# A graph layer's own features, stored to DRAM and added by block in place of a transposed copy

## The reference

```
h = relu(layernorm(x)); x = x + layer0(h)   # edge-weighted sum over neighbours, then two linear maps
h = relu(layernorm(x)); x = x + layer1(h)

# layer1(feat):
m = relu(feat[src]) + EPS
a = exp(m - segment_max) / segment_sum(exp)     # softmax over the edges that end in a node, per feature
msg = segment_sum(a * m, dst)
return (feat + msg) @ W + b
```

## Time and profile before

| | us |
|---|---|
| median of 3 runs | 2506.68 (2506.21 to 2509.19) |
| the profiled execution | 2505.36 |
| its span, first to last instruction | 2503.60 |
| mean granted clock of TensorE | 0.874 of full speed |
| busy: TensorE, VectorE, GpSimd, ScalarE | 1874.7, 1846.6, 1503.2, 772.3 |
| moved to and from DRAM | 332.03 MB, mean 133 GB/s |

### The profile page before, as it was taken

How to read it: one execution, slowest core, us unless ns; L and a number is a source line. 1 busy time by engine, 2 the same in 40 slices (tenths; PEclk the granted TensorE clock), 3 DMA queues, 4 the chain that set the end, 5 groups by cost and what they waited for, 6 DMA issues and landing times.

```text
span 2503.6 us, 54920 instructions
## 1 busy us (share of the span) xinstructions
PE 1874.7 (75%) x11673; PEld 1561.1 (62%) x11674; DVE 1846.6 (74%) x4248; ACT 772.3 (31%) x1316; POOL 1503.2 (60%) x1556
## 2 busy tenths in 40 slices
PE   3777777776676767577676776776667677999999
PEld 2466666665565656466565665655555566888887
DVE  8999998878787888778787878887877883222232
ACT  5001121222233333344444444445445552000000
POOL 4777777777777777777777777777777600000000
PEclk9899898888888888888888888788888878999999
DMA  5234344444444444454544445454455424656553
GB/s 160 50 83 105 94 116 104 115 114 110 124 114 117 120 119 125 117 143 118 138 124 134 130 131 145 136 136 138 135 134 139 121 79 170 216 195 213 203 205 134
DMA packets 150484, 332.03 MB, mean 133 GB/s; under 512 B 58051, under 2 KB 108253, under 8 KB 134446
## 3 DMA queue, kind: packets, MB, share of 16 engines
q1 hardware_dynamic: 29758, 166.84, 22.3%
q0 software_dynamic: 49248, 75.74, 13.7%
q10 hardware_dynamic: 71258, 87.51, 10.2%
HBM read 242.47 MB, written 87.48 MB: 132 GB/s over the span
## 4 chain that ended last, share of the span: by engine, by line
POOL 55%; PE 19%; issue 19%; DMA 3%; DVE 3%; ACT 1%; POOLq 0%; DVEq 0%; ACTq 0%; SPq 0%
POOL rows_buf L522 55%; PE ps L775 16%; DMA rows_buf<-table,index 2%; PE ps L608 1%; DVE ps L1216 1%; ACT features_buf L838 0%; PE ps L700 0%; PE ps L597 0%; PE ps L789 0%; DVE zone L1330 0%; DVE zone L1253 0%; PE ps L754 0%; DMA xs<-x 0%; PE ps L783 0%; POOLq L527 0%
## 5 line engine op out<-in xcount | busy, mean ns | idle before, releaser
L522 POOL DMA_INDIRECT rows_buf<-table,index x1539 | 1488.0, 967 | 495.6 <-issue 491.9
L700 PE MATMUL ps<-zone,planes 128*128 128x400 f16 x2352 | 614.9, 377 | 537.1 <-DVE zone L1253 425.8
L1253 DVE TENSOR_SCALAR zone<-iota_c,planes 128x400 f16<-128x400 int16 x2352 | 673.0, 339 | 59.9 <-issue 49.1
L896 ACT ACTIVATE features_buf<-ps 128x800 f16<-128x800 f32 x392 | 327.8, 836 | 1214.6 <-PE ps L700 1209.3
L700 PEld LDWEIGHTS ps<-zone,planes 128*128 128x128 f16 x2352 | 251.1, 107 | 715.3 <-issue 657.8
L597 PEld LDWEIGHTS ps<-wet,zone 128*128 128x128 f32 x3136 | 543.7, 248 | 43.8 <-issue 32.4
L597 PE MATMUL ps<-wet,zone 128*128 128x96 f32 x3136 | 530.6, 327 | 8.5 <-DMA zone<-edge_t 8.5
L584 PE MATMUL ps<-onehot,features_buf 128*96 128x128 f32 x3120 | 421.2, 280 | 0.0
L584 PEld LDWEIGHTS ps<-onehot,features_buf 128*96 128x96 f32 x3120 | 387.4, 171 | 11.2 <-issue 1.1
L1216 DVE TENSOR_TENSOR ps<-ps,rows_buf 128x768 f32<-128x768 f32 x171 | 164.5, 962 | 240.1 <-DMA rows_buf<-table,index 211.0
L1018 DVE TENSOR_TENSOR planes<-ps,planes 128x1536 f16<-128x1536 f32 x196 | 341.2, 1741 | 0.0
(11 more groups left out here) (162 smaller groups left out, 595.7 us busy)
## 6 DMA issues: line engine op xcount, KB each, us to landing
counts<-features_buf ACTq DMA_DIRECT2D x392, 200.0 KB
zone<-edge_t SPq DMA_DIRECT2D x98, 768.0 KB
rows_buf<-counts SPq DMA_DIRECT2D x32, 1600.0 KB, 6.3
single<-table SPq DMA_DIRECT2D x3072, 0.4 KB
planes<-counts SPq DMA_DIRECT2D x17, 1600.0 KB, 6.2
rows_buf<-table,index POOLq DMA_INDIRECT x1539
final<-residual ACTq DMA_DIRECT2D x48, 48.0 KB, 3.5
out<-final ACTq DMA_DIRECT2D x48, 48.0 KB, 3.9
```

Of the source, the lines that this page charges most:

```text
L522: nc.gpsimd.indirect_dma_start(out=into[:, t, :], out_offset=None, in_=table, in_offset=bass.IndirectOffsetOnAxis(ap=at[:, t:t + 1], axis= ...
L700: nc.tensor.matmul(count_ps[:, bass.ds(banks[k], WC)], row_hot[:, u % 2, g * GS + k, :], pair_hot[:, g * GS + k, :], start=False, stop=Fal ...
L896: nc.scalar.activation(count_out[:, k], bank, ACT.Copy, accum_out=row_sum[:, bass.ds(p, 1)]).then_inc(moved, 1)
L1253: last = nc.vector.tensor_scalar(pair_hot[:, k, :], iota_c[:, :], step_pair[:, bass.ds(i * (IS * SC) + (u * SC + k), 1)], None, ALU.is_equal)
```

## The change

In the fast branch the 50 transposes and 20 copies of the second layer are dropped (they move into the other branch, which does not run here). Instead SyncE stores `hs`, unit by unit, to a new DRAM tensor `hidden`, behind the store of the residual. VectorE waits for these stores (`own_out`) before L1337, since it overwrites `hs`. ScalarE waits for them too, and for the last count step, and loads a block of `hidden` ahead of each block of the residual into `own`, six buffers in a zone that is free by then. VectorE adds it in `softmax` in a new operation, ahead of the transpose, and the operation that takes the turned result out of PSUM is a plain copy.

```
+                for u in range(NU):
+                    sp.wait_ge(features, NU + u + 1)
+                    for part in (slice(0, EVEN), slice(EVEN, NP)):
+                        sp.dma_start(hidden.rearrange("(p j) d -> p j d", j=NJ)[part, units[u], :],
+                                     hs[part, units[u], :]).then_inc(own_out, 16)
                 sp.wait_ge(parts_ready, 1)
...
             node_layer(hidden_out, N // UC, uT, w2s, 0)
-            pe.wait_ge(node_out, NG)
-            transposes(1)
 
             with pe.If(fast_of(pe) > 0):
-                pe.wait_ge(turned_out, 2 * NG)
+                pe.wait_ge(node_out, NG)
                 pe.wait_ge(parts_ready, 3)
...
                 def residual_load(b, u, rows_at, n=P):
+                    act.dma_start(own[0:n, u % BU, :], hidden[rows_at, :]).then_inc(own_in[u % BU], 16)
                     act.dma_start(final[0:n, u % BU, :], residual[rows_at, :]).then_inc(residual_in[u % BU], 16)
...
                 act.wait_ge(residual_out, 32)
+                act.wait_ge(own_out, 2 * NU * 16)
+                act.wait_ge(step_done, SC + NSTEP)
...
-            for g in range(NG):
-                dve.wait_ge(turned, NG + g + 1)
-                for into, group in turned_group(h1t[0:D, 0:N], g):
-                    last = nc.vector.tensor_copy(into, group)
-                last.then_inc(turned_out, 1)
             with dve.If(fast_of(dve) > 0):
                 chain = chained(fast_step)
 
                 dve.wait_ge(fexp_ready, 1)
-                dve.wait_ge(turned_out, 2 * NG)
+                dve.wait_ge(own_out, 2 * NU * 16)
                 nc.vector.scalar_tensor_tensor(hs[:, :, :], hs[:, :, :], P_SCALE, sq, ALU.mult,
                                                ALU.mult).then_inc(weighted_ready, 1)
...
                     nc.vector.scalar_tensor_tensor(soft[:, slot, 3, 0:D], total, 1.0 / P_SCALE,
                                                    soft[:, slot, 2, D:2 * D], ALU.mult, ALU.mult
-                                                   ).then_inc(soft_done, 1)
+                                                   ).then_inc(soft_step[5], 1)
+                    dve.wait_ge(soft_step[5], b + 1)
+                    dve.wait_ge(own_in[u % BU], (i + (u // BU + 1)) * 16)
+                    nc.vector.tensor_tensor(soft[:, slot, 3, 0:D], soft[:, slot, 3, 0:D], own[:, u % BU, :], ALU.add
+                                            ).then_inc(soft_done, 1)
...
-                    nc.vector.tensor_tensor(node_t[0:D, slot, :], h1t[0:D, bass.ds(b * P, P)], ps[0:D, 2 + slot, 0:P],
-                                            ALU.add).then_inc(soft_added, 1)
+                    nc.vector.tensor_copy(node_t[0:D, slot, :], ps[0:D, 2 + slot, 0:P]).then_inc(soft_added, 1)
```

More of the change, by code:

```diff
@@ L65 @@
 BU = 6
+FEAT = 5760
 FIRST = 2
@@ L110, in gnn_kernel @@
     residual = nc.dram_tensor("residual", (N, D), F32, kind="Internal").ap()
+    hidden = nc.dram_tensor("hidden", (N, D), F32, kind="Internal").ap()
     counts = nc.dram_tensor("counts", (P, NWIN, WC), F16, kind="Internal").ap()
@@ L222, in gnn_kernel @@
         h1t = zone[0:D + 1, 0:NB * P]
+        own = zone[:, FEAT:FEAT + BU * D].rearrange("p (u d) -> p u d", u=BU)
         table16 = planes[:, 0:NJ * 2 * D].bitcast(F16).rearrange("p (j d) -> p j d", j=NJ)
@@ L328, in gnn_kernel @@
         soft_turned = sem("soft_turned")
-        soft_step = [sem(f"soft_step{k}") for k in range(5)]
+        soft_step = [sem(f"soft_step{k}") for k in range(6)]
         soft_added = sem("soft_added")
@@ L332, in gnn_kernel @@
         residual_out = sem("residual_out")
+        own_out = sem("own_out")
+        own_in = [sem(f"own_in{u}") for u in range(BU)]
         residual_in = [sem(f"residual_in{u}") for u in range(BU)]
@@ L810, in _ @@
             with pe.Else():
+                pe.wait_ge(node_out, NG)
+                transposes(1)
                 with pe.Fori(0, NC // NS) as i:
@@ L1344, in _, with softmax @@
                                             ALU.subtract).then_inc(rest_ready, 1)
-                def softmax(b, slot):
+                def softmax(b, u, i):
+                    slot = u % 2
                     total, weight = soft[:, slot, 0, 0:D], soft[:, slot, 0, D:2 * D]
@@ L1381, in add_final @@
                     nc.vector.tensor_tensor(to, to, ps[0:n, 4 + u % 2, 0:D], ALU.add).then_inc(final_ready, 1)
-                softmax(0, 0)
-                softmax(1, 1)
+                softmax(0, 0, 0)
+                softmax(1, 1, 0)
                 add_aggregate(0, 0)
@@ L1387, in _ @@
                     for u in range(FIRST, FIRST + BU):
-                        softmax(i * BU + u, u % 2)
+                        softmax(i * BU + u, u, i)
                         add_aggregate(i * BU + (u - 1), (u - 1) % 2)
@@ L1391, in _ @@
                 for b in range(LAST, NB):
-                    softmax(b, b % 2)
+                    softmax(b, b, 0)
                     add_aggregate(b - 1, (b - 1) % 2)
@@ L1399, in _ @@
                 chain = chained(general_step)
+                for g in range(NG):
+                    dve.wait_ge(turned, NG + g + 1)
+                    for into, group in turned_group(h1t[0:D, 0:N], g):
+                        last = nc.vector.tensor_copy(into, group)
+                    last.then_inc(turned_out, 1)
                 for half in range(2):
```

## The result

| | before | after |
|---|---|---|
| median, us | 2507.42 (7 runs, 2505.72 to 2512.93) | 2518.57 (7 runs, 2515.04 to 2526.74) |
| ratio of the times | | 1.0043, 95% interval 1.0032 to 1.0055 |
| profiled execution, us | 2505.36 | 2521.62 |
| its span, us | 2503.60 | 2519.7 |

The change costs 10.8 us (2507.42 x 0.0043; the interval is 8 to 13.8). The forecast was 7.3 us, and 2514.0 with a range up to 2517.0: the sign and the place are right, the size is too small. In some executions further down both kernels, before and after, took some 1200 us longer, in every trace taken of them ahead of the passage and for a reason that stays open; each is compared only with the kernel before that stands beside it.

The account below looks back on a forecast made before the run. Bound: GpSimd's gathers (untouched), then the pass chain from L1337 into TensorE's block sums. Stores' wait 7.0 plus last-block tail 0.3 gave +7.3 us on the 2506.68 median: 2514.0, range 2510.8 to 2517.0.

Parts of the forecast that it names:

- The bound, and the place of the change: From L1337 to TensorE's first block sum, 18.75 us without slack; whatever moves L1337 moves the end by as much.
- Part 1: Before L1337, 50 transposes and 20 copies leave the fast path: gain at most 1.5 to 1.6 us.
- The missing warm-up: TensorE's first block sums, without the dropped transposes that had lifted its clock: cost 0.
- Part 2: L1337 waits for features' stores behind SyncE's queue: 2062.5 + 7.0 + 0.5 = 2070.0, so 7.0 us later.
- Its last part: What the changed profile would show, including VectorE idle to 2070 and DMA share near 1 until 2069.5.
- Part 3: ScalarE's 49 more loads of 48 KB, own features block by block, hidden behind TensorE: 0, bounds 0 to 2 us.
- Rival C: Block 0's small loads land too late, over 20 us, so the stage slips 1 to 4 us more; chance 3%.
- Part 4: One more add per softmax, exposed only in the last block: +0.3 us, bounds 0.25 to 0.4.
- A (overlap): Features' stores overlap the queue ahead, cost only 4 to 5 us: 2510.7 to 2511.7; chance 10%.
- B (landed before the exponentials): Before L1337, stores land before the exponentials end at 2061.4: -1.2 us, 2505.5; chance 3%.
- D: General path runs, so the wait is not reached; same or slower by a few us; chance 2% with unforeseen gathers move.

Follow-up runs that it names:

- none: Changed kernel without the second layer's own features (no stores, loads, wait or add); first pass 11.85 us after the flag; 2506.86 us against 2507.63 for the kernel before.
- hid_first: Changed kernel with SyncE issuing the features' stores ahead of block 0 and the residual; first pass at 11.86 us; 3719.65 us against 3719.77 before, ratio 1.0003.
- hid_early: Changed kernel with the features' stores issued before SyncE reads the flag, as units become ready; first pass at 11.85 us; 2507.69 us against 2507.63 before, ratio 0.9999.
- after_again: The changed kernel traced a second time, nothing altered; first pass 24.32 us after the flag; 3738.31 us against 3719.77 for the kernel before.
- spread: Changed kernel with the 13-row DMAs of residual and features reading spread partitions, writing to spare tensors; first pass 22.04 us after the flag; 2522.82 us against 2509.80 before.
- stores: No graph layer: only x loaded and stored, with groups of the disputed stores, each waited for; 13 adjacent rows 3.06 us, 13 spread 0.83.
- stores_more: No graph layer, further groups: L block load; R, r residual's 112 and 13 rows; H, h features' likewise; the whole takes 21.9 and 22.7 us.
- rest_last: Changed kernel with the residual's last 13 partitions stored behind the features; first pass 20.97 us after the flag; 3728.62 us against 3719.77 for the kernel before.

## Why the prediction was wrong in size and right in kind

**The bound, and the place of the change: right.** L1345 moves and everything after it by as much, 18.75 us in every trace.

**Part 1, right.** The possible gain from the transposes and copies was put at 1.5 to 1.6 us; with the wait gone it is 1.62 to 1.63 against the first trace of before and 1.84 to 1.85 against the second (none, hid_first, hid_early). The missing warm-up was costed at 0, and no trace speaks against it.

**Part 2, the step that failed.** That SyncE's queue decides, that issue is no limit (the ten stores took 8.58 us to issue, longer than the forecast had, and it did not matter), and that the wait ends some 0.5 us after the last data: all as forecast (the last packet ends at 2077.93 and L1345 starts at 2078.40). One reading was wrong by itself: 2062.5, or 12.96 us after the flag, is where the last of the first 4.0 MB start; in the kernel before they end at 2063.61. The term that was mis-sized is the time of the stores behind 2062.5: 7.0 us in the sum, bounds 5.7 to 8.5. Measured: 25.08 - 12.96 - 0.5 = 11.6 us, and 10.9 in after_again. It falls into two parts:
- The stores by themselves. With adjacency taken out (spread) the term is 22.04 - 12.96 - 0.5 = 8.6 us. This is about the upper bound of the prediction, the rate of 281 GB/s at the kernel's head. The 7.0 came from a window of 1.25 us at full share, 326 GB/s, and from mean engine time. In stores the 112 even rows of the features take 7.2 us, and their 13 rest rows add 1.3 to 1.8, of which their bytes at the same rate are 0.8: 9.0 together. So 1.6 us of the error lie in the choice of 7.0, with a right value at the edge of the bounds.
- The residual's last 13 rows, which the prediction counted with the 4.0 MB ahead as done at 2062.5. In the kernel before they end by 2063.61, with nothing behind them. With 2.4 MB behind them they slow to as much as 4.55 us a packet (5.03 in after_again), and the last ends at 2070.42. Spreading the 13-row DMAs gives 2.3 to 3.0 us of it back. Without the graph layer (stores_more) the presence of r costs 2.3 and 3.2 us (L R H h against L R r H h), of which spreading gives back 1.3 to 1.9. This was outside the bounds, and no rival had it: each looked at whether the stores behind could move early, none at whether they would slow down what stands ahead.

The two parts make up the whole term, 10.9 to 11.6 us, by the way they are split. The packet records say where the time goes. From the features' first packet to their last, in the mean of 16 engines, after has 12.1 us = 6.6 of features + 2.35 of residual rows + 3.1 of nothing (and 0.1 of small packets); spread has 9.1 = 6.75 + 0.7 + 1.5; rest_last has 8.6 = 6.5 + 1.6 + 0.3. The features' engine time hardly moves, and as engine time the forecast's 7.0 was nearly right. What it left out is the rest: slow rows that hold engines, and engines that run empty one after the other behind them. With 16 packets in flight at a time, one for each of 16 engines, a slow row takes a place that a feature packet would have; that each of the 13 rows goes to an engine of its own fits this and the 13 that start within 0.42 us in stores, but the records do not name the engine. Why the rows slow down when the features are behind them stays open, and so does why rest_last gave back 3.4 to 4.1 us in the kernel where stores has 2.3 to 2.5 and stores_more 2.3 to 3.2.

**Where the reading went wrong.** The prediction took the share of 0.99 as proof that a queue's end is known from bytes and mean rate. Its last part expected "DMA engines at a share near 1 until 2069.5". All engines did have a packet until 2070.5, but for 2.35 us of that mean they were at the residual's rows; and then it took another 7.4 us until the last of them was done. A mean of 16 engines hides that some have finished and one has not, and a share booked where packets start hides when they end.

**Part 3, right.** Own loads cost nothing. DMA issues from the page of after (KB each, median us to landing; the first line answers to nothing before, the second to the earlier trace rows):
```profile
zone<-hidden ACTq DMA_DIRECT2D x48, 48.0 KB, 3.3
final<-residual ACTq DMA_DIRECT2D x48, 48.0 KB, 3.0
```
The first four of each, issued beside 3.2 MB of block loads, landed after 8.0 and 7.7 us, where 18 was the fear. Rival C falls: no block waited, and the period is still 8.44 us (8.434 to 8.437 from the third block on, as in before).

**Part 4, right.** Groups by line from 2126 to 2496 (answers to the earlier trace rows), and the last block in order of time:
```profile
L1361 DVE COPY soft<-ps 128x192 f32<-128x192 f32 x44 | 15.7, 358 | 244.8 <-PE ps L783 244.8
...
L1387 DVE COPY node_t<-ps 96x128 f32<-96x128 f32 x44 | 12.3, 279 | 0.0
L1382 DVE TENSOR_TENSOR soft<-soft,zone 128x96 f32<-128x96 f32 x44 | 11.4, 259 | 2.9
```
```profile
2514.75 0.26 DVE L1377 SCALAR_TENSOR_TENSOR soft<-soft 128x96 f32<-128x96 f32 x1
2515.04 0.26 DVE L1382 TENSOR_TENSOR soft<-soft,zone 128x96 f32<-128x96 f32 x1
...
2515.36 0.31 PE L791 MATMUL ps<-ident,soft 128*96 128x128 f32 x1 [2.27 <-DVE soft L1382]
```
The new add takes 0.259 us and no load delays it; VectorE's idle time before the softmax shrinks by 13.9 us in 44 blocks (from 258.7), which is about the add with the idle time beside it (11.4 + 2.9). From L1377 to the last transpose's start it is 0.61 us, against 0.32 before: +0.3, as forecast. The two rows of before:
```profile
2498.67 0.26 DVE L1368 SCALAR_TENSOR_TENSOR soft<-soft 128x96 f32<-128x96 f32 x1
...
2498.99 0.31 PE L783 MATMUL ps<-ident,soft 128*96 128x128 f32 x1 [1.97 <-DVE soft L1368]
```

**The rivals.** A (overlap) would have put the pass 2 to 3 us earlier than the forecast, and it came later. B (landed before the exponentials) needs the stores out of the queue's end; put at its head they are, and that is hid_first. D: the change does what it says.

## What to carry to other kernels

A store whose source is overwritten soon belongs at the head of its queue, not behind transfers that nobody waits for yet: here the order alone was worth 12.5 to 13.2 us of the passage and 11 us of the measured time, more than six times what the removed work could bring. And do not take the end of a busy DMA queue from bytes and a mean share: look for the DMAs with few partitions in it (a remainder of 13 adjacent partitions cost 2.3 to 3.2 us for a sixteenth of the bytes ahead), since the wait ends with the last packet, and ask what the new transfers do to those that stand ahead of them.

## What the runs showed of the hardware that was not expected

- Thirteen rows of 19,200 bytes from adjacent partitions: 3.06 us (82 GB/s). From spread ones: 0.83 us (301 GB/s).
- The same thirteen rows cost 0.7 us at a queue's end and 2.4 to 2.8 us with 2.2 MB queued behind them, and their slowest packet goes from 1.5 or 1.6 to 4.0 or 4.1 us, so a transfer is slowed by what is issued after it.
- With 16 DMA engines full the packets in flight number 16, and a packet that takes 4.55 us in place of 0.71 leaves fewer of them to the rest: 3.1 of 12.1 us of engine time were idle in the mean while one wait was still open.
